# A shifted-window transformer block: the first score pass loads its queries and its block-diagonal keys from the second pass's pages in DRAM

## The chip, the cores and the metric

The kernel runs on one core of a Trainium2 chip. The metric is the device time of one launch in microseconds (us). The engines are TensorE (PE, with its weight loads as PEld), VectorE (DVE), ScalarE (ACT), GpSimd (POOL) and SyncE (SP), which here issues every DMA. There are 16 DMA engines, and all of SP's DMAs go into one queue.

## The reference

The input is a batch of 32 images of 96 channels and 56 x 56 pixels, in float32. One Swin block is computed:

```
f = layernorm(x over channels) * g1 + b1, rolled by (-3, -3)
win = windows of 7 x 7 = 49 tokens            (64 windows per image)
q, k, v = win @ w_qkv + b_qkv                 (12 heads of 8 channels)
attn = softmax(q k^T / sqrt(8) + mask)        (mask: -100 between regions of the rolled image)
f = x + roll back(attn v @ w_proj + b_proj)
out = f + gelu((layernorm(f) * g2 + b2) @ w_fc1 + b_fc1) @ w_fc2 + b_fc2
```

## The kernel before

**Bands and steps.** A band is one row of 8 windows, 392 tokens (`TOK`). There are 256 bands. Work is software-pipelined by hand: in step t each stage works on band t plus its own offset (line 60): `LOAD` 9, `ORDER` 7, `TURN` 6, `BACK` 5, `QK` 4, `KEYS` 3, `VALUES`, `SCORE` and `STACK` 2, `PROB` 0, `WEIGH` -1. Every engine runs its own list of stages per step, one list for odd and one for even t (`step` of each engine), and engines meet only at semaphores. A loop of 32 steps runs seven times, and the other steps are written out (`steps`, line 181).

**Two score passes.** Scores are computed twice. The first pass (`scores`, L404 to L421; PSUM banks from A) has query tokens in rows and key tokens in columns and multiplies high fp16 parts only; the DVE takes row maxima from it (`maxima`, L736). The maxima are transposed, and ACT copies them to `mrow` (L650), which a DMA writes into one row of `qbd`. The second pass (`shifted`, L423 to L437; banks from B) has key tokens in rows. It multiplies stacked high and low parts and subtracts mask and maximum in the same matmul. ACT exponentiates its result (L623), and `weighted` (L439) multiplies it with `vbd`.

A matmul covers a quad of 4 heads and one window at a time: 49 query tokens against 4 x 49 key columns. Heads are kept apart by a block-diagonal operand: in `kbd` the rows of head h are non-zero only in the columns of head h. In the first pass of before the stationary operand is `nat`: 96 channel rows of queries, and 4 mask rows from 96 on. `kbd` has the same 96 rows and 4 mask rows for 12 heads. Both are 128 partitions deep with zeros for the rest.

**From projections to score operands.** `queries_keys` (PE, L495) leaves q and k of band t+4 in PSUM. ACT writes the high parts to `nat` at the end of step t (`queries_keys_high`, L638 to L644, semaphore `qk_high`). The DVE writes the low parts (`queries_keys_low`, L778, `qk_low`): in an odd step as the third operation, in an even one after the first maximum, each time for the band of the step before. SP then writes them to DRAM in `save_parts` (L283): L292 the high keys into the diagonal of the zeroed image `k_image` (DRAM, two of them), L293 both parts of q and k into `stack_pages`, and L294 the high parts a second time, so that a stack of 3 pieces per channel (high, low, high or high, high, low) stands in each page. In the next step `key_blocks` (L258) waits for the image and loads it whole into `kbd` (L264: 96 rows of 9,408 bytes, zeros with it), for `scores` one step later. `stacks` (L266) loads `kst` and `qbd` from `stack_pages` for the second pass.

**SP's order in a step** is `load_x` (L256), `key_blocks` (L264), in odd steps two `store_y` (L300), then `stacks` (L272, and L274 four times), `maxima` (L281), `save_parts` (L292 to L294). SP works through it in order; the wait for `qk_low` in `save_parts` is for the DVE of the following step. `alone` (L203) only counts.

**PE's order** is in `step` (L567). In an odd step `shifted`(0) and `values` (L400) stand before `scores`(0); in an even step `scores`(0) is first. `scores`(0) waits for `key_in` (L409).

**Start.** The DVE zeroes the operand tiles (L703 to L709), then SP loads constants (L224; 28 DMAs, among them two writes of zeroed `kbd` to the images at L243), and all engines wait for the last of them.

Of the kernel before, what the change touches and what calls it, by code (L numbers as in the profile page):

```python
# [31 lines left out]
F16 = mybir.dt.float16  # L32
# [5 lines left out]
HD = C // NH  # L38
# [11 lines left out]
MASK0, MAXROW = C, C + 4  # L50
CH = 4 * L
# [11 lines left out]
N_CONST = 9 + 5 + 6 + 5 + 3  # L63
# [28 lines left out]
def build(nc, x, g1, b1, wqkv, bqkv, wproj, bproj, g2, b2, wfc1, bfc1, wfc2, bfc2,  # L92
# [7 lines left out]
    with ctx:  # L100
# [24 lines left out]
        nat = sb("nat", [FULL, 5, 4, TOK], F16)  # L125
        kst = sb("kst", [FULL, 3, QUADS, TOK], F16)
        qbd = sb("qbd", [FULL, 2, NH, TOK], F16)
        kbd = sb("kbd", [FULL, 2, NH, TOK], F16)
        vbd = sb("vbd", [FULL, 4, PAIRS * NH, 2, HD + 1])
# [17 lines left out]
        parts_out = [stack_pages[n, TOK:TOK + 2 * side].rearrange("(s c m t) -> c s m t", s=2, m=3, t=TOK)[:, :, 0:2, :] for n in range(4)]  # L147
        high_out = [stack_pages[n].rearrange("(s r) -> s r", s=2)[:, 0:side].rearrange("s (c m t) -> c s m t", m=3, t=TOK)[:, :, 0, :] for n in range(4)]
        k_pages = nc.dram_tensor("k_image", [2, NH, HD * NH * TOK + TOK], F16, kind="Internal").ap()
        k_image = [k_pages[n].rearrange("h r -> (h r)")[0:C * NH * TOK].rearrange("(c g t) -> c g t", g=NH, t=TOK) for n in range(2)]  # L150
        k_diagonal = [k_pages[n, :, 0:HD * NH * TOK].rearrange("h (d r) -> h d r", d=HD)[:, :, 0:TOK] for n in range(2)]
# [7 lines left out]
        image_out = [sem(f"image_out{n}") for n in range(2)]  # L159
# [4 lines left out]
        NAT_OUT, STACK_IN = 2 * 16, 5 * 16  # L164
# [42 lines left out]
        def nat_slot(b):  # L207
            return 4 if b.last() else b.c % 4

        def kst_slot(b):  # L210
            return 2 if b.last() else b.c % 2
# [10 lines left out]
        def _(sp):  # L222
# [19 lines left out]
            for n in range(2):  # L242
                const(k_image[n], kbd[0:C, n, :, :])  # L243
                const(kbd[MASK0:MAXROW, n, :, :], rows_d[2, 0:4])
                const(qbd[MASK0:MAXROW, n, :, :], rows_d[2, 0:4])
            for n in range(5):
                const(nat[MASK0:MAXROW, n, 0, :], rows_d[n // 4, 0:4, 0, :])
            for n in range(3):
                const(kst[MASK0:MAXROW + 1, n, :, :], rows_d[n // 2, :, 0:QUADS, :])
# [8 lines left out]
            def key_blocks(b):  # L258
                n = b.c % 2
                wait(sp, s_made, b.count(QUADS, -QUADS))  # L260
                alone(sp)
                sp.wait_ge(image_out[n], b.used(2, 16))
                alone(sp)
                sp.dma_start(kbd[0:C, n, :, :], k_image[n]).then_inc(key_in[n], 16)  # L264

            def stacks(b):  # L266
# [3 lines left out]
                sp.wait_ge(nat_out[n], b.used(4, NAT_OUT))  # L270
                alone(sp)
                sp.dma_start(kst[0:C, kst_slot(b), :, :], k_stack[n].rearrange("(c a) m t -> (a m) c t", c=QUADS)).then_inc(stack_in[n], 16)  # L272
# [10 lines left out]
            def save_parts(b):  # L283
# [3 lines left out]
                wait(sp, key_in[b.c % 2], b.step(-2).used(2, 16))  # L287
                alone(sp)
                sp.wait_ge(qk_low, b.count(1, 1))
                alone(sp)  # L290
                parts = nat[0:C, nat_slot(b), :, :]
                sp.dma_start(k_diagonal[b.c % 2], parts[:, 2, :]).then_inc(image_out[b.c % 2], 16)  # L292
                sp.dma_start(parts_out[n], parts.rearrange("c (s m) t -> c s m t", s=2)).then_inc(nat_out[n], 16)  # L293
                sp.dma_start(high_out[n], parts[:, 0:4:2, :]).then_inc(nat_out[n], 16)  # L294
# [76 lines left out]
        def _(pe):  # L371
# [32 lines left out]
            def scores(t, u):  # L404
# [3 lines left out]
                if u == 0:  # L408
                    pe.wait_ge(key_in[b.c % 2], b.used(2, 16))  # L409
# [6 lines left out]
                for p in range(PAIRS):  # L416
                    for w in range(2):
                        toks = slice((2 * p + w) * L, (2 * p + w + 1) * L)
                        last = nc.tensor.matmul(psum[W1 * w:W1 * w + L, A + p // 2, p % 2 * CH:(p % 2 + 1) * CH],  # L419
                                                nat[:, nat_slot(b), 0, toks], kbd[:, b.c % 2, 4 * u:4 * u + 4, toks], start=True, stop=True)  # L420
# [452 lines left out]
```

## Time and profile before

| | before |
|---|---|
| three runs | 3273.74, 3298.38, 3312.33 us |
| median | 3298.38 us |
| the profiled execution | 3292.7 us, its span 3290.8 us |
| busy: PE, PEld, DVE, ACT, POOL | 89%, 71%, 74%, 63%, 44% |
| mean granted clock of TensorE, of full speed | 0.977 |
| DMA moved | 573.07 MB |
| loads of `kbd` | 256 of 882.0 KB, 6.8 us median from issue to landing |

Busy is the time in which an engine executed at least one instruction, as a share of the span. Waits of the bottleneck engine are what a change can take away. The profiled execution has its own time; sums over its rows are made against 3292.7 us.

### The profile page before, as it was taken

The numbers are of one execution on the slowest core, as the hardware profiler recorded it, in microseconds if no ns is written. First come the engines' busy times: TensorE is split into PE (matmuls) and PEld (weight loads), VectorE is DVE, ScalarE is ACT, GpSimd is POOL, SyncE is SP. The second block draws the span as 40 slices with busy tenths as digits, with TensorE's granted clock in tenths as the row PEclk, the third lists the DMA queues.
The fourth block names the chain that finished last, engine by engine and source line by source line (L and its number), as shares of the span: only waits on it lengthen the run. The fifth ranks groups of instructions, "written<-read, shape, count | busy, mean of one in ns | idle before, by whom it ended". The sixth has DMA issues, their size and how long they took to land.

```text
span 3290.8 us, 136960 instructions
## 1 busy us (share of the span) xinstructions
PE 2926.7 (89%) x53060; PEld 2338.7 (71%) x53060; DVE 2430.1 (74%) x7208; ACT 2070.5 (63%) x3208; POOL 1453.1 (44%) x1832
## 2 busy tenths in 40 slices
PE   1789999899998899989998999989999899999997
PEld 0677777777776777767776777767777777777775
DVE  5677777677776777767777777767777677777775
ACT  0366666566666666656666666666666566666664
POOL 2444444344444444444444444444444444444444
PEclk9799999899999999999999999999999999999999
DMA  1667777677776777767777777767767677777772
GB/s 40 170 170 187 182 190 188 164 172 184 185 175 171 176 183 193 186 164 186 189 180 175 177 178 194 184 164 186 187 168 186 164 188 179 188 186 192 182 183 71
DMA packets 409846, 573.07 MB, mean 174 GB/s; under 512 B 58376, under 2 KB 384350, under 8 KB 384365
## 3 DMA queue, kind: packets, MB, share of 16 engines
q1 hardware_dynamic: 409148, 563.72, 68.9%
q8 instruction: 444, 7.27, 1.0%
q14 instruction: 254, 2.07, 0.2%
HBM read 385.92 MB, written 175.21 MB: 171 GB/s over the span
## 4 chain that ended last, share of the span: by engine, by line
PE 40%; DMA 26%; issue 11%; SPq 10%; DVE 9%; ACT 4%; POOL 0%; DVEq 0%; POOLq 0%; ACTq 0%
DMA kbd<-k_image 24%; PE psum L451 10%; PE psum L384 9%; PE psum L419 5%; PE psum L435 4%; PE psum L492 4%; PE psum L477 4%; DVE nat L778 3%; DVE nmax L736 3%; ACT xfh L635 3%; SPq L292 2%; SPq L256 2%; SPq L293 2%; SPq L294 2%; PE psum L527 2%
## 5 line engine op out<-in xcount | busy, mean ns | idle before, releaser
L623 ACT ACTIVATE probs<-psum 113x784 f32<-113x784 f32 x768 | 632.2, 823 | 847.4 <-PE psum L435 844.2
L736 DVE TENSOR_REDUCE nmax<-psum 113x16 f32<-113x784 f32 x768 | 745.6, 971 | 316.5 <-PE psum L419 316.2
L347 POOL TENSOR_SCALAR ve<-mv 98x8 f32<-98x8 f32 x264 | 64.1, 243 | 1687.7 <-DVE mv L765 1687.7
L451 PE MATMUL psum<-vbd,probs 128*49 128x18 f32 x24576 | 656.5, 199 | 26.3 <-issue 25.5
L451 PEld LDWEIGHTS psum<-vbd,probs 128*49 128x49 f32 x24576 | 646.0, 128 | 32.0 <-issue 31.7
L419 PE MATMUL psum<-kbd,nat 128*49 128x196 f16 x6144 | 412.5, 254 | 114.5 <-DMA kbd<-k_image 103.8
L435 PE MATMUL psum<-qbd,kst 128*49 128x196 f16 x6144 | 413.7, 254 | 67.0 <-DVE xfl L771 45.5
L354 POOL TENSOR_TENSOR rs<-ve,half 98x8 f32<-98x8 f32 x264 | 439.5, 1665 | 0.0
L760 DVE BATCH_NORM_STATS2 st<-tok 98x6 f32<-98x96 f32 x2112 | 363.7, 245 | 80.8 <-ACT tok L630 67.3
L359 POOL TENSOR_TENSOR xn<-xn,rs 98x768 f32<-98x768 f32 x264 | 387.8, 1469 | 72.7 <-POOL rs L354 72.7
L419 PEld LDWEIGHTS psum<-kbd,nat 128*49 128x49 f16 x6144 | 269.4, 105 | 209.2 <-DMA kbd<-k_image 134.4
L771 DVE TENSOR_TENSOR xfl<-psum,xfh 96x784 f16<-96x784 f32 x264 | 256.1, 970 | 190.5 <-ACT xfh L635 188.5
L350 POOL TENSOR_TENSOR xn<-tok,mv 98x768 f32<-98x768 f32 x264 | 389.1, 1474 | 0.2 <-POOL ve L347 0.2
L435 PEld LDWEIGHTS psum<-qbd,kst 128*49 128x49 f16 x6144 | 243.4, 105 | 166.5 <-issue 129.8
L564 PE MATMUL psum<-hid,w 128*96 128x392 f32 x1024 | 359.7, 494 | 0.9 <-ACT hid L666 0.9
L644 ACT ACTIVATE nat<-psum 96x784 f16<-96x784 f32 x256 | 209.7, 819 | 129.2 <-PE psum L384 129.2
L564 PEld LDWEIGHTS psum<-hid,w 128*96 128x96 f32 x1024 | 167.5, 164 | 171.8 <-issue 170.5
L492 PE MATMUL psum<-ident,xn 98*96 98x98 f32 x2112 | 228.0, 252 | 65.3 <-issue 57.4
L617 ACT ACTIVATE vbd<-psum 49x384 f32<-49x384 f32 x512 | 261.0, 510 | 10.8 <-PE psum L400 4.4
L635 ACT ACTIVATE xfh<-psum 96x784 f16<-96x784 f32 x264 | 215.2, 815 | 78.6 <-PE psum L492 78.3
L492 PEld LDWEIGHTS psum<-ident,xn 98*96 98x96 f32 x2112 | 189.6, 128 | 91.4 <-issue 81.6
L666 ACT ACTIVATE hid<-psum 96x784 f32<-96x784 f32 x256 | 209.8, 819 | 60.5 <-PE psum L384 55.7
(83 smaller groups left out, 5343.1 us busy)
## 6 DMA issues: line engine op xcount, KB each, us to landing
kbd<-k_image SPq DMA_DIRECT2D x256, 882.0 KB, 6.8
stack_pages<-nat SPq DMA_DIRECT2D x256, 294.0 KB, 3.0
kst<-stack_pages SPq DMA_DIRECT2D x256, 220.5 KB
qbd<-stack_pages SPq DMA_DIRECT2D x1024, 55.1 KB
stack_pages<-nat SPq DMA_DIRECT2D x256, 147.0 KB, 3.7
xr<-in_x_dram SPq DMA_DIRECT2D x224, 147.0 KB, 3.6
out_dram<-yr SPq DMA_DIRECT2D x224, 147.0 KB, 6.3
k_image<-nat SPq DMA_DIRECT2D x256, 73.5 KB
```

Of the source, the lines that this page charges most:

```text
L350: nc.gpsimd.tensor_tensor(xn[:, n, :, :], tok[:, n, :, :, :].rearrange("t k p c -> t (k p) c"), mv[:, n, :, 0:1].to_broadcast(wide_by_toke ...
L354: nc.gpsimd.tensor_tensor(rs[:, n, :], ve[:, n, :], half[0:PT, :], ALU.pow).then_inc(root_done, 1)
L359: nc.gpsimd.tensor_tensor(xn[:, n, :, :], xn[:, n, :, :], rs[:, n, :].rearrange("t (g a) -> t g a", a=1).to_broadcast(wide_by_token), ALU. ...
L419: last = nc.tensor.matmul(psum[W1 * w:W1 * w + L, A + p // 2, p % 2 * CH:(p % 2 + 1) * CH], nat[:, nat_slot(b), 0, toks], kbd[:, b.c % 2, ...
L435: last = nc.tensor.matmul(psum[W1 * w:W1 * w + L, B + p // 2, p % 2 * CH:(p % 2 + 1) * CH], kst[:, kst_slot(b), u, toks], qbd[:, b.c % 2, ...
L451: last = nc.tensor.matmul(dst[:, :, h, :], probs[:, b.c % 2, h // 4, p, h % 4 * L:(h % 4 + 1) * L], vbd[:, b.c % 4, p * NH + h, :, :], sta ...
L492: last = nc.tensor.transpose(psum[0:C, B + kind, p * PT:(p + 1) * PT], xn[:, b.c % 2, kind * PAIRS + p, :], ident[0:PT, 0:PT])
L564: last = nc.tensor.matmul(psum[0:C, D + n, 0:TOK], w2[:, m, :], hid[:, b.c % 2, m, :], start=m == 0, stop=m == 1)
L623: nc.scalar.activation(probs[0:PR, b.c % 2, u, :, :].rearrange("j (g q) k -> j g (q k)", g=2), psum[0:PR, B:B + 2, 0:2 * CH], ACT.Exp).the ...
L635: nc.scalar.activation(xfh[0:C, b.c % 4, :, :], psum[0:C, B:B + 2, 0:TOK], ACT.Copy).then_inc(n_high, 1)
L736: nc.vector.tensor_reduce(dst, psum[0:PR, A:A + 2, 0:2 * CH].rearrange("i g (q h j) -> i g q h j", q=2, j=L), axis=AX.X, op=ALU.max, negat ...
L760: last = nc.vector.bn_stats(st[:, n, g, :], tok[:, n, g // PAIRS, g % PAIRS, :])
```

## The change

The first pass works on the 32 channel rows of one quad. A new tile `qst` (3 slots x 3 quads) holds in rows 0 to 31 the high queries of a quad, and in rows 32 to 35 (`QUAD` is 32) the mask rows. `kbd` keeps its shape, but rows 0 to 31 hold the four diagonal blocks of each quad. The image of key blocks in DRAM, its zeroing at the start, its write in each step and its load are gone. Instead `key_blocks` reads the high parts from `stack_pages`: one DMA for `qst` (73.5 KB) and four for `kbd` (8 rows x 3 quads, 18.4 KB each). The matmuls have the same number, shape and depth (128 rows).

`save_parts` issues the write of the high parts when `qk_high` has come, and then waits for `qk_low` to write both parts. `key_blocks` waits for the write of the high parts only (`high_out`). `nat` has 4 slots instead of 5 and no mask rows. ACT's write of `nat` no longer waits for scores, since no matmul reads `nat`. The start has 24 constant DMAs.

```diff
@@ -122,10 +123,11 @@
         st, mv = sb("st", [PT, 2, 2 * PAIRS, 6]), sb("mv", [PT, 2, 2 * PAIRS, 2])
         ve, rs = sb("ve", [PT, 2, 2 * PAIRS]), sb("rs", [PT, 2, 2 * PAIRS])
         xfh, xfl = sb("xfh", [FULL, 4, 2, TOK], F16), sb("xfl", [FULL, 4, 2, TOK], F16)
-        nat = sb("nat", [FULL, 5, 4, TOK], F16)
+        nat = sb("nat", [C, 4, 4, TOK], F16)
         kst = sb("kst", [FULL, 3, QUADS, TOK], F16)
         qbd = sb("qbd", [FULL, 2, NH, TOK], F16)
         kbd = sb("kbd", [FULL, 2, NH, TOK], F16)
+        qst = sb("qst", [FULL, 3, QUADS, TOK], F16)
         vbd = sb("vbd", [FULL, 4, PAIRS * NH, 2, HD + 1])
         nmax = sb("nmax", [PR, 2, NH * PAIRS])
         mrow = sb("mrow", [NH * PAIRS, 2, PT], F16)
...
@@ -144,11 +146,8 @@
         stack_pages = nc.dram_tensor("stack_pages", [4, 2 * (side + 3 * TOK)], F16, kind="Internal").ap()
         q_stack = [stack_pages[n, 0:side].rearrange("(c m t) -> c m t", m=3, t=TOK) for n in range(4)]
         k_stack = [stack_pages[n, TOK + side:TOK + 2 * side].rearrange("(c m t) -> c m t", m=3, t=TOK) for n in range(4)]
-        parts_out = [stack_pages[n, TOK:TOK + 2 * side].rearrange("(s c m t) -> c s m t", s=2, m=3, t=TOK)[:, :, 0:2, :] for n in range(4)]
-        high_out = [stack_pages[n].rearrange("(s r) -> s r", s=2)[:, 0:side].rearrange("s (c m t) -> c s m t", m=3, t=TOK)[:, :, 0, :] for n in range(4)]
-        k_pages = nc.dram_tensor("k_image", [2, NH, HD * NH * TOK + TOK], F16, kind="Internal").ap()
-        k_image = [k_pages[n].rearrange("h r -> (h r)")[0:C * NH * TOK].rearrange("(c g t) -> c g t", g=NH, t=TOK) for n in range(2)]
-        k_diagonal = [k_pages[n, :, 0:HD * NH * TOK].rearrange("h (d r) -> h d r", d=HD)[:, :, 0:TOK] for n in range(2)]
+        both_parts = [stack_pages[n, TOK:TOK + 2 * side].rearrange("(s c m t) -> c s m t", s=2, m=3, t=TOK)[:, :, 0:2, :] for n in range(4)]
+        high_parts = [stack_pages[n].rearrange("(s r) -> s r", s=2)[:, 0:side].rearrange("s (c m t) -> c s m t", m=3, t=TOK)[:, :, 0, :] for n in range(4)]
 
         consts_in, filled, rows_one, vbd_zero, vbd_ones = sem("consts_in"), sem("filled"), sem("rows_one"), sem("vbd_zero"), sem("vbd_ones")
         psum_clear, weights_wide, weights_high, weights_set = sem("psum_clear"), sem("weights_wide"), sem("weights_high"), sem("weights_set")
...
@@ -156,12 +155,12 @@
 
         x_in = [sem(f"x_in{n}") for n in range(8)]
         nat_out = [sem(f"nat_out{n}") for n in range(4)]
-        image_out = [sem(f"image_out{n}") for n in range(2)]
+        high_out = [sem(f"high_out{n}") for n in range(4)]
         key_in = [sem(f"key_in{n}") for n in range(2)]
         stack_in = [sem(f"stack_in{n}") for n in range(4)]
         max_in = [sem(f"max_in{n}") for n in range(2)]
         y_out = [sem(f"y_out{n}") for n in range(8)]
-        NAT_OUT, STACK_IN = 2 * 16, 5 * 16
+        STACK_IN, KEY_IN = 5 * 16, 5 * 16
         X_IN = [16] * 7 + [2 * 16]
 
         passed = sem("passed")
...
@@ -204,10 +203,7 @@
 
             engine.sem_inc(passed, 1)
 
-        def nat_slot(b):
-            return 4 if b.last() else b.c % 4
-
-        def kst_slot(b):
+        def masked_slot(b):
             return 2 if b.last() else b.c % 2
 
         def odd(t):
...
@@ -240,12 +236,10 @@
                 column(n, v)
 
             for n in range(2):
-                const(k_image[n], kbd[0:C, n, :, :])
-                const(kbd[MASK0:MAXROW, n, :, :], rows_d[2, 0:4])
+                const(kbd[QUAD:QUAD + 4, n, :, :], rows_d[2, 0:4])
                 const(qbd[MASK0:MAXROW, n, :, :], rows_d[2, 0:4])
-            for n in range(5):
-                const(nat[MASK0:MAXROW, n, 0, :], rows_d[n // 4, 0:4, 0, :])
             for n in range(3):
+                const(qst[QUAD:QUAD + 4, n, :, :], rows_d[n // 2, 0:4, 0:QUADS, :])
                 const(kst[MASK0:MAXROW + 1, n, :, :], rows_d[n // 2, :, 0:QUADS, :])
             sp.wait_ge(consts_in, 16 * N_CONST)
 
...
@@ -259,17 +253,20 @@
                 n = b.c % 2
                 wait(sp, s_made, b.count(QUADS, -QUADS))
                 alone(sp)
-                sp.wait_ge(image_out[n], b.used(2, 16))
-                alone(sp)
-                sp.dma_start(kbd[0:C, n, :, :], k_image[n]).then_inc(key_in[n], 16)
+                sp.wait_ge(high_out[b.c % 4], b.used(4, 16))
+                alone(sp)
+                sp.dma_start(qst[0:QUAD, masked_slot(b), :, :], q_stack[b.c % 4].rearrange("(c a) m t -> m a c t", c=QUADS)[0]).then_inc(key_in[n], 16)
+                for h in range(4):
+                    sp.dma_start(kbd[HD * h:HD * (h + 1), n, h:NH:4, :],
+                                 k_stack[b.c % 4].rearrange("(c h d) m t -> h m d c t", c=QUADS, h=4)[h, 2]).then_inc(key_in[n], 16)
 
             def stacks(b):
                 n = b.c % 4
                 wait(sp, p_made, b.count(QUADS, -QUADS))
                 alone(sp)
-                sp.wait_ge(nat_out[n], b.used(4, NAT_OUT))
-                alone(sp)
-                sp.dma_start(kst[0:C, kst_slot(b), :, :], k_stack[n].rearrange("(c a) m t -> (a m) c t", c=QUADS)).then_inc(stack_in[n], 16)
+                sp.wait_ge(nat_out[n], b.used(4, 16))
+                alone(sp)
+                sp.dma_start(kst[0:C, masked_slot(b), :, :], k_stack[n].rearrange("(c a) m t -> (a m) c t", c=QUADS)).then_inc(stack_in[n], 16)
                 for h in range(4):
                     sp.dma_start(qbd[HEAD * h:HEAD * (h + 1), b.c % 2, h:NH:4, :],
                                  q_stack[n].rearrange("(c h d) m t -> h (d m) c t", c=QUADS, h=4)[h]).then_inc(stack_in[n], 16)
...
@@ -284,14 +281,12 @@
                 n = b.c % 4
                 wait(sp, stack_in[n], b.step(-4).used(4, STACK_IN))
                 alone(sp)
-                wait(sp, key_in[b.c % 2], b.step(-2).used(2, 16))
-                alone(sp)
+                sp.wait_ge(qk_high, b.count(1, 1))
+                alone(sp)
+                sp.dma_start(high_parts[n], nat[:, n, 0:4:2, :]).then_inc(high_out[n], 16)
                 sp.wait_ge(qk_low, b.count(1, 1))
                 alone(sp)
-                parts = nat[0:C, nat_slot(b), :, :]
-                sp.dma_start(k_diagonal[b.c % 2], parts[:, 2, :]).then_inc(image_out[b.c % 2], 16)
-                sp.dma_start(parts_out[n], parts.rearrange("c (s m) t -> c s m t", s=2)).then_inc(nat_out[n], 16)
-                sp.dma_start(high_out[n], parts[:, 0:4:2, :]).then_inc(nat_out[n], 16)
+                sp.dma_start(both_parts[n], nat[:, n, :, :].rearrange("c (s m) t -> c s m t", s=2)).then_inc(nat_out[n], 16)
 
             def store_y(b):
                 sp.wait_ge(y_made, b.count(1, 1))
...
@@ -406,7 +401,7 @@
                 if not has(b):
                     return
                 if u == 0:
-                    pe.wait_ge(key_in[b.c % 2], b.used(2, 16))
+                    pe.wait_ge(key_in[b.c % 2], b.used(2, KEY_IN))
                     if odd(t):
                         if has(t.step(QK - 1)):
                             pe.wait_ge(qk_low, t.step(QK - 1).count(1, 1))
...
@@ -417,7 +412,7 @@
                     for w in range(2):
                         toks = slice((2 * p + w) * L, (2 * p + w + 1) * L)
                         last = nc.tensor.matmul(psum[W1 * w:W1 * w + L, A + p // 2, p % 2 * CH:(p % 2 + 1) * CH],
-                                                nat[:, nat_slot(b), 0, toks], kbd[:, b.c % 2, 4 * u:4 * u + 4, toks], start=True, stop=True)
+                                                qst[:, masked_slot(b), u, toks], kbd[:, b.c % 2, 4 * u:4 * u + 4, toks], start=True, stop=True)
                 last.then_inc(s_made, 1)
 
             def shifted(t, u):
...
@@ -638,10 +633,9 @@
                 b = t.step(QK)
                 at = D if odd(t) else A
                 act.wait_ge(qk_made, b.count(1, 1))
-                wait(act, nat_out[b.c % 4], b.step(-4).used(4, NAT_OUT))
-                wait(act, image_out[b.c % 2], b.step(-4).used(2, 16))
-                wait(act, s_made, b.count(QUADS, -3 * QUADS))
-                nc.scalar.activation(nat[0:C, nat_slot(b), 0:4:2, :], psum[0:C, at:at + 2, 0:TOK], ACT.Copy, scale=1 / GAIN).then_inc(qk_high, 1)
+                wait(act, nat_out[b.c % 4], b.step(-4).used(4, 16))
+                wait(act, high_out[b.c % 4], b.step(-4).used(4, 16))
+                nc.scalar.activation(nat[0:C, b.c % 4, 0:4:2, :], psum[0:C, at:at + 2, 0:TOK], ACT.Copy, scale=1 / GAIN).then_inc(qk_high, 1)
 
             def max_rows(t):
                 b = t.step(SCORE)
...
@@ -699,9 +693,9 @@
         @block.vector
         def _(dve):
 
-            for a in (kbd, qbd):
+            for a in (kbd, qbd, qst):
                 nc.vector.memset(a[:, :, :, :], 0.0)
-            for a in (wide, wide1, wp, w2, xfh, xfl, oT, hid, nat, kst, probs):
+            for a in (wide, wide1, wp, w2, xfh, xfl, oT, hid, kst, probs):
                 last = nc.vector.memset(a[FILL:FULL], 0.0)
             last.then_inc(filled, 1)
             dve.wait_ge(filled, 1)
```

## Rows read from the trace of the kernel before

**Rows 1.** The page: span and busy time of each engine
```profile
span 3290.8 us, 136960 instructions
PE 2926.7 (89%) x53060; PEld 2338.7 (71%) x53060; DVE 2430.1 (74%) x7208; ACT 2070.5 (63%) x3208; POOL 1453.1 (44%) x1832
```

**Rows 2.** Waits, whole span: total us, times, longest us
```profile
PE psum L419 <- DMA kbd<-k_image: 103.8, 111, 3.3
PE psum L435 <- DVE xfl L771: 45.5, 10, 6.7
```

**Rows 3.** Waits of SP's own queue, whole span
```profile
SPq L205 <- DVE nat L778: 736.7, 256, 17.6
SPq L205 <- ACT mrow L650: 182.8, 118, 4.0
SPq L205 <- DMA k_image<-nat: 112.0, 97, 3.1
```

**Rows 4.** Timeline of an even step and the next odd one: start us, us, instruction
```profile
1526.11 0.82 ACT L644 ACTIVATE nat<-psum 96x784 f16<-96x784 f32 x1 [0.18 <-PE psum L384]
1528.59 0.96 DVE L778 SCALAR_TENSOR_TENSOR nat<-psum,nat 96x784 f16<-96x784 f32 x1
1529.64 0.80 SPq L292 DMA_DIRECT2D k_image<-nat  x1
1530.49 0.51 SPq L293 DMA_DIRECT2D stack_pages<-nat  x1
1531.83 0.34 SPq L256 DMA_DIRECT2D xr<-in_x_dram  x1
1532.43 0.33 SPq L264 DMA_DIRECT2D kbd<-k_image  x1
1536.82 0.58 SPq L281 DMA_DIRECT2D qbd<-mrow  x1
1539.33 0.21 PE L400 MATMUL psum<-wl,xfh 128*49 128x96 f16 x2
1539.86 0.53 PE L419 MATMUL psum<-kbd,nat 128*49 128x196 f16 x8 [0.32 <-DMA kbd<-k_image]
...
1550.14 0.53 PE L419 MATMUL psum<-kbd,nat 128*49 128x196 f16 x8
```

**Rows 5.** Instructions of L274, L264 and L292: nanoseconds, least, median, most
```profile
L274 SPq DMA_DIRECT2D qbd<-stack_pages x1024: 291/427/1636, 97.8 to 3234.1; - x171
L264 SPq DMA_DIRECT2D kbd<-k_image x256: 303/320/1361, 84.5 to 3221.1; - x128
L292 SPq DMA_DIRECT2D k_image<-nat x256: 770/797/892, 81.9 to 3218.8; - x128
```

**Rows 6.** Issue to landing: first L264, then L294, then L256
```profile
DMA to landing us min/median/max: 5.8/6.8/8.9
DMA to landing us min/median/max: 2.8/3.7/5.7
DMA to landing us min/median/max: 1.8/3.3/6.0
```

**Rows 7.** Timeline of the start: start, duration
```profile
17.71 3.33 DVE L705 MEMSET nat<- 32x3920 uint32 x1 [0.77 <-issue]
33.76 0.43 SPq L224 DMA_DIRECT2D k_image<-kbd  x1
35.61 1.47 SPq L224 DMA_DIRECT2D k_image<-kbd  x1
38.81 2.98 SPq L224 DMA_DIRECT2D nat<-in_rows_dram  x5
41.83 0.97 SPq L224 DMA_DIRECT2D kst<-in_rows_dram  x3
```

**Rows 8.** Windows: start:end, length, PE busy, granted clock, DMA share, GB/s
```profile
200.00:3000.00 2800.00, 2566.34 (x46977) 0.98 0.73 181
2400.00:2412.50 12.50, 11.02 (x187) 0.73 0.89 220
```

More of the change, by code:

```diff
@@ L50 @@
 MASK0, MAXROW = C, C + 4
+QUAD = C // QUADS
 CH = 4 * L
@@ L62 @@
 HIDDEN, RESULT, STORE = (-5, -4), (-6, -5), (-7, -6)
-N_CONST = 9 + 5 + 6 + 5 + 3
+N_CONST = 9 + 5 + 4 + 6
 class Band:
@@ L435, in shifted @@
                         last = nc.tensor.matmul(psum[W1 * w:W1 * w + L, B + p // 2, p % 2 * CH:(p % 2 + 1) * CH],
-                                                kst[:, kst_slot(b), u, toks], qbd[:, b.c % 2, 4 * u:4 * u + 4, toks], start=True, stop=True)
+                                                kst[:, masked_slot(b), u, toks], qbd[:, b.c % 2, 4 * u:4 * u + 4, toks], start=True, stop=True)
                 last.then_inc(p_made, 1)
@@ L776, in queries_keys_low @@
                 dve.wait_ge(qk_high, b.count(1, 1))
-                parts = nat[0:C, nat_slot(b), :, :]
+                parts = nat[0:C, b.c % 4, :, :]
                 nc.vector.scalar_tensor_tensor(out=parts[:, 1:4:2, :], in0=psum[0:C, at:at + 2, 0:TOK], scalar=1 / GAIN, in1=parts[:, 0:4:2, :],
```

## The prediction, made before the changed kernel ran

> **What bounds the kernel now.** I read the busy times first: PE is busy 2926.7 of 3290.8 us, and DVE, the next, 2430.1 [rows 1]. So PE sets the time, and only its 364.1 us of idleness and its own work can change the result. The change leaves PE's work alone: as many matmuls of the same shape over the same 128 rows. So I read what PE waited for [rows 2]. The largest single item is the load of `kbd`, 103.8 us in 111 waits, 0.94 us each. The 45.5 us in 10 waits for the DVE's low parts, up to 6.7 us each, are mostly the seven loop returns, and stay. What PE has at stake here is 103.8 us, 3.2% of the span.
>
> Then the timeline around one such wait [rows 4]. ACT has the high parts of band t+4 at 1526.93. The DVE has the low parts at 1529.55. Only then does SP write: the image write takes 0.80 us to issue, the page write 0.51, then come the second high write and the load of x, and the load of `kbd` goes out at 1532.43. It lands at about 1539.82, when PE has been free since 1539.54. The chain from low parts to landed keys is 10.3 us against 10.0 us that PE's own work lasts. SP's waits [rows 3] say the same from the other side: 112.0 us in 97 waits are spent on the image write's landing, before the big load can even be issued.
>
> **The change, part by part.**
>
> Removed and added in SP's queue, per band. The image write goes (0.797 us median) and the `kbd` load (0.320) [rows 5]. Five loads come. For each of the four `kbd` pieces the nearest row is L274, also one of four DMAs that each take one head in four out of these pages: 0.427 us median, 0.291 to 1.636 [rows 5]; I take the median. For `qst`, a load of all its rows at once, I take the 0.320 of L264. New issue 4 x 0.427 + 0.320 = 2.03 us against 1.12 removed, so +0.91 us per band, and about 0.05 us between issues for three more DMAs, as between the rows of the timeline: +1.06 us, 271 us over 256 bands. SP's three largest waits sum to 1031.5 us [rows 3], so this is covered: SP stays idle for over 700 us. If that cover were gone, all of it would be paid, see the third rival.
>
> The load, timed on the rows 4. High parts: ready at 1526.93, SP is waiting, write issued at about 1527.0, landed by 3.7 us later (L294's median; 2.8 to 5.7) [rows 6] at 1530.7. Low parts at 1529.55; page write issued 1529.64 to 1530.15. From its end to the load of x now pass 0.83 us with L294's issue in them; I keep them whole, so x goes out at 1530.98 to 1531.32, and `key_blocks` starts near 1531.6 (0.26 us on, as now). The high write has landed by then, so the new wait costs nothing. The last of the five loads is issued at 1531.6 + 0.37 + 3 x 0.48 = 1533.4. Its landing is not in the trace. Bounds: 1.8 us, the fastest load of x, and 8.9, the slowest of the whole image [rows 6]. I take 3.3, the median of the x loads, which carry 147.0 KB each, as much as the five together. Landed at 1536.7, against 1539.54 when PE arrives: 2.8 us spare, where now 0.3 are missing. With the 6.8 of today's load it would be 1540.2 and as late as now; with 8.9, 2.8 us late. In the even steps SP is busy longer: the maxima go out at 1536.82 for 0.58 [rows 4], in future about 1 us later, so the high write is issued near 1538.4 and lands at 1542.1. There the high write is the last to come, and `key_blocks` waits for it. The last load is issued near 1543.9 and lands at 1547.2, against PE's even scores at 1550.14. So both parities have 2.8 us spare or a little more. Queued behind that wait are in odd steps the stores, the stacks and the maxima; none is due before the step after next.
>
> Term 1: the waits for `kbd`, -103.8 us. What stays of them: at the seven loop returns SP itself is late, and a wait there can outlast the cover. I leave 7 times half of the longest wait (3.3), 12 us. Bounds: all 103.8 gained, or none. I take -92.
>
> Behind PE's wait nothing else was hidden that I can find: in the odd step the DVE's maxima come as PE's scores end, where the DVE is idle until PE delivers; PE does `weighted` in between.
>
> Traffic. 882.0 KB and 73.5 KB per band become 147.0 KB. DMA engines are busy 0.73 of the time [rows 8] and would fall well below 0.6. PE does not wait for bandwidth as such, so I count nothing for that; the instruction fetch, which may profit, is in a rival.
>
> Term 2: the start [rows 7]. The DVE's memset of `nat` goes (3.33 + 0.77 us), and one of `qst` comes, 1.5 us by its 1764 words against 3920. SP issues two image writes less (0.43 + 1.47), five masks of `nat` less (2.98) and three of `qst` more (0.97 by `kst`). That is -2.6 and -3.9 us, all on the path, since every engine waits for the last constant. Two image writes less in the queue are worth 0 to 3 us. Sum -6.5 to -9.5, I take -7.
>
> Term 3: the clock. Its mean is 0.98 over 2800 us [rows 8]: 4% of the time at 1.2 instead of 2.4 GHz, 112 us, costing at most 56. Most low stretches follow the loop returns; the one at 2400 does not [rows 8]. Bounds 0 and -56; PE's waits for `kbd` are 29% of its idleness and short, so I take -5.
> The Trainium skill (TensorE: Matmul & The Clock Gate, "HAM oscillation — how this bites in real kernels") says that waits for DMA between bursts of matmuls throttle the clock again, after which work runs at half rate. Read that way, the low stretches would be a price of waits like these, and the sum would use up to all of the 56 us: that is the second rival. The trace speaks for little of it, as 111 such waits go with few low stretches.
>
> **Sum:** 3292.7 - 92 - 7 - 5 = 3189 us. The profiled execution (3292.7) lies 0.2% under the median of the three runs (3298.38), which go from 3273.74 to 3312.33; I let the sum stand for the new median.
>
> **Rivals.**
>
> *The loads land as late as now.* Five DMAs behind the page write of 294 KB instead of one: their fixed parts count, not their bytes. It needs a landing of over 6.1 us after the last issue. For it: 6.8 is what the load has today, and x loads have taken 6.0. Against it: it moves a sixth of the bytes. Then only the start is gained: 3292.7 - 7 = 3286. The Trainium skill (DMA: Bandwidth & Descriptors, "Measured", under Bandwidth) advises to batch DMAs to 1 MiB and calls transfers under 64 KB descriptor-dominated, which speaks for this rival; x's small loads, at 3.3 us, speak against. Chance 0.12.
>
> *More than the waits.* Less idleness keeps the clock up, and lighter queues shorten the instruction fetch stalls. 3292.7 - 104 - 9 - 40 = 3140, the 40 being most of the clock's 56. Chance 0.10.
>
> *SP becomes the bound.* It holds every DMA, and if the four small loads cost more than L274's, SP uses up its 1031 us. What it may spend per piece: per band it has 1031.5 / 256 = 4.03 us idle and 1.12 us removed, and gives 0.32 for `qst` and 0.15 between issues; the other 4.68 us over four pieces are 1.17 us each. Above that each 0.1 us costs 102 us over 1024 pieces: at 1.4 us the time would be 3292.7 - 7 + 236 = 3522. For it: issues of 1.36 and 1.64 us do occur, and the waits in SP's queue can't all be moved to where they are needed. Against: the median is 0.427. With partial queueing the result is merely slower by a few per cent. Chance 0.08, slower.
>
> *Half is given back.* PE, no longer held, meets the DVE's first or second maximum of the odd step or a fetch stall that the wait had covered. 3292.7 - 52 - 7 = 3234. Chance 0.12.
>
> **Numbers.** The forecast, 3189 us, has 0.58. Range: the low end is the second rival less a quarter of the spread of the three runs (38.6 us), 3130; the high end is the half gain plus 1% for runs, 3266. That leaves out the first and third rival. Within 1% of the median, 3265 to 3331, is what I can't tell from no change. Faster: 0.58 + 0.12 + 0.10 = 0.80; same 0.12; slower 0.08.
>
> **What would show it.** Right: PE's wait for `kbd` or `qst` under 20 us in total; SP's waits still over 600 us, with no large one for the high write; the last `kbd` load lands 3 to 4 us after its issue; first matmul of the constants near 40 us instead of 47.5; DMA bytes near 359 MB (573 less 256 times 955.5 KB and plus 256 times 147 KB, at 1,024 bytes a KB, less the two images at the start). Wrong: a landing over 6 us; L264's successors with a median issue over 1 us; PE's waits for the maxima of L736 in place of those for the keys; a mean clock under 0.97.

## The result and the profile after

| | before | after |
|---|---|---|
| median | 3292.15 us (4 runs, 3273.74 to 3312.33) | 3062.89 us (4 runs, 3061.32 to 3065.84) |
| span of the profiled execution | 3290.8 us | 3061.1 us |
| mean granted clock | 0.977 | 0.992 |
| DMA moved | 573.07 MB | 359.37 MB |

The ratio is 0.9303, with a 95% interval of 0.9246 to 0.9361. The change is worth 229 us, more than twice the 109 us of the forecast, and lies under the low end of the range. Medians here are over all runs of a kernel, ratios over its fast ones alone (within 1.5% of its fastest), which leaves out one run each of e1_bulk and e10_bulk_half, five of the ten of e9_bulk_first, and two of the thirteen of before that go with e9 to e11.

The page after, span and busy time, as in [rows 1]:

```profile
span 3061.1 us, 137479 instructions
PE 2862.6 (94%) x53060; PEld 2299.2 (75%) x53060; DVE 2424.3 (79%) x7208; ACT 2076.6 (68%) x3208; POOL 1454.5 (48%) x1832
```

PE's idle time went from 364.1 to 198.5 us, and its busy time fell by 64.1 us, for the same 53060 matmuls. The chain that ended last now is PE for 87% of the span.

PE's waits after (total us, times, longest us), which answer to [rows 2], and its stalls, which stand mostly within groups of equal matmuls:

```profile
PE psum L371 <- DMA kst<-in_rows_dram: 38.1, 1, 38.1
PE psum L487 <- issue: 57.1, 120, 1.0
PE psum L430 <- DVE xfl L765: 23.2, 10, 2.8
PE psum L446 <- issue: 9.0, 18, 1.0
PE psum L414 <- issue: 4.2, 7, 2.5
PE psum L430 <- issue: 2.8, 5, 0.7
```

The same view before had, beside [rows 2]:

```profile
PE psum L376 <- DMA kst<-in_rows_dram: 47.5, 1, 47.5
PE psum L492 <- issue: 57.4, 121, 1.0
PE psum L451 <- issue: 25.5, 38, 1.5
PE psum L435 <- issue: 12.3, 19, 2.1
PE psum L419 <- issue: 6.6, 9, 1.5
PE psum L400 <- issue: 1.7, 4, 0.7
```

(L451, L435, L419 and L400 of before are L446, L430, L414 and L395 after.) No wait for keys is left, and three other things became smaller. "Issue" in the middle of a group of equal matmuls is no semaphore, since the program has none there: PE waits for nothing but its own next instruction. ("Issue" at the head of a group, as in L487, can be a semaphore that the profile did not match; e7_back_early shows that one to be such.) SP's own waits after:

```profile
SPq L204 <- DVE nat L772: 473.9, 254, 5.4
SPq L204 <- ACT nat L638: 222.7, 166, 15.0
SPq L204 <- ACT mrow L644: 167.1, 115, 3.0
SPq L204 <- DMA stack_pages<-nat: 5.8, 13, 0.9
```

They still sum to 869.5 us, and the new wait for the high write costs 5.8. Against [rows 4], the timeline of an even step (start, duration):

```profile
1498.21 0.32 SPq L286 DMA_DIRECT2D stack_pages<-nat  x1
1499.45 0.96 DVE L772 SCALAR_TENSOR_TENSOR nat<-psum,nat 96x784 f16<-96x784 f32 x1
1500.51 0.30 SPq L289 DMA_DIRECT2D stack_pages<-nat  x1
1501.15 1.23 SPq L250 DMA_DIRECT2D xr<-in_x_dram  x1
1502.64 0.30 SPq L258 DMA_DIRECT2D qst<-stack_pages  x1
1502.99 1.36 SPq L260 DMA_DIRECT2D kbd<-stack_pages  x4
...
1510.09 0.51 PE L414 MATMUL psum<-kbd,qst 128*49 128x196 f16 x8
```

The loads are all issued at 1504.35, 5.7 us before PE begins the scores. The last step of their semaphore that the trace has comes at 1505.74, 1.4 us after the last issue. The four pieces of `kbd` cost 0.300 us each to issue and the high write lands in 2.0 us; L260, and then the landing of L286:

```profile
L260 SPq DMA_DIRECT2D kbd<-stack_pages x1024: 264/300/1815, 73.9 to 2989.7; - x171
DMA to landing us min/median/max: 1.9/2.0/4.2
```

One loop return in each kernel, from the DVE's side: the first instruction of the DVE after it, with its idle time in brackets, before and after.

```profile
1412.26 0.62 DVE L785 SCALAR_TENSOR_TENSOR f<-psum,vec,xw 96x392 f32<-96x392 f32 x1 [7.26 <-issue]
934.50 0.62 DVE L779 SCALAR_TENSOR_TENSOR f<-psum,vec,xw 96x392 f32<-96x392 f32 x1 [3.40 <-issue]
```

PE waits at L435 (L430 after) for this DVE: 6.0 to 6.7 us at each of the six returns of before, 2.5 to 2.8 after.

Two windows (start:end, length, PE busy, granted clock, DMA share, GB/s), as in [rows 8]:

```profile
200.00:3000.00 2800.00, 2704.58 (x50651) 1.00 0.47 122
2400.00:2412.50 12.50, 9.88 (x185) 0.86 0.29 74
```

**Where the 229.7 us of the spans went:**

| | before | after | gain |
|---|---|---|---|
| wait for keys | 103.8 | 0 | 103.8 |
| L435, now L430, waiting for the DVE's low parts, six long ones at loop returns | 45.5 | 23.2 | 22.3 |
| "issue" stalls in L451, L435, L419 and L400 | 46.1 | 16.0 | 30.1 |
| first matmul of the start | 47.5 | 38.1 | 9.4 |
| PE's other idle time (the rest of 364.1 and 198.5) | 121.2 | 121.2 | 0 |
| PE busy | 2926.7 | 2862.6 | 64.1 |

The waits for keys, which I had forecast, are less than half.

### The profile page after: what moved, and what is told of

It is laid out like the page before. It is cut to its first block, busy times and chain, and to the rows that moved or that the text cites. A ratio compares the mean times of both kernels' runs of the same rounds, so it can differ in the third digit from the quotient of the medians.

```text
span 3061.1 us, 137479 instructions
## 1 busy us (share of the span) xinstructions
PE 2862.6 (94%) x53060; PEld 2299.2 (75%) x53060; DVE 2424.3 (79%) x7208; ACT 2076.6 (68%) x3208; POOL 1454.5 (48%) x1832
## 2 busy tenths in 40 slices
DMA packets 414727, 359.37 MB, mean 117 GB/s; under 512 B 63455, under 2 KB 413985, under 8 KB 414012
## 3 DMA queue, kind: packets, MB, share of 16 engines
q1 hardware_dynamic: 414028, 350.01, 43.7%
## 4 chain that ended last, share of the span: by engine, by line
PE 87%; issue 5%; ACT 5%; DVE 2%; POOL 1%; SPq 0%; DMA 0%; POOLq 0%; DVEq 0%; ACTq 0%
PE psum L446 18%; PE psum L379 16%; PE psum L559 11%; PE psum L430 10%; PE psum L414 8%; PE psum L472 7%; PE psum L487 6%; PE psum L532 5%; ACT probs L618 4%; PE psum L522 3%; PE psum L395 2%; PE psum L511 1%; DVE st L754 1%; POOL rs L349 0%; DVE xfl L765 0%
## 5 line engine op out<-in xcount | busy, mean ns | idle before, releaser
L446 PE MATMUL psum<-vbd,probs 128*49 128x18 f32 x24576 | 644.2, 198 | 9.8 <-issue 9.0
L446 PEld LDWEIGHTS psum<-vbd,probs 128*49 128x49 f32 x24576 | 634.4, 126 | 14.1 <-issue 13.3
L430 PE MATMUL psum<-qbd,kst 128*49 128x196 f16 x6144 | 405.1, 251 | 36.3 <-DVE xfl L765 23.2
L414 PE MATMUL psum<-kbd,qst 128*49 128x196 f16 x6144 | 401.4, 250 | 7.6 <-issue 4.2
L430 PEld LDWEIGHTS psum<-qbd,kst 128*49 128x49 f16 x6144 | 238.8, 104 | 142.1 <-issue 103.0
L414 PEld LDWEIGHTS psum<-kbd,qst 128*49 128x49 f16 x6144 | 265.0, 104 | 85.3 <-issue 80.6
L559 PEld LDWEIGHTS psum<-hid,w 128*96 128x96 f32 x1024 | 167.4, 164 | 171.9 <-issue 170.6
L487 PE MATMUL psum<-ident,xn 98*96 98x98 f32 x2112 | 227.8, 252 | 64.9 <-issue 57.1
L487 PEld LDWEIGHTS psum<-ident,xn 98*96 98x96 f32 x2112 | 189.3, 128 | 91.0 <-issue 81.1
L772 DVE SCALAR_TENSOR_TENSOR nat<-psum,nat 96x784 f16<-96x784 f32 x256 | 245.7, 960 | 0.0
## 6 DMA issues: line engine op xcount, KB each, us to landing
qst<-stack_pages SPq DMA_DIRECT2D x256, 73.5 KB
kbd<-stack_pages SPq DMA_DIRECT2D x1024, 18.4 KB
```

The lines of the kernel that those rows point to most:

```text
L430: last = nc.tensor.matmul(psum[W1 * w:W1 * w + L, B + p // 2, p % 2 * CH:(p % 2 + 1) * CH], kst[:, masked_slot(b), u, toks], qbd[:, b.c % ...
L446: last = nc.tensor.matmul(dst[:, :, h, :], probs[:, b.c % 2, h // 4, p, h % 4 * L:(h % 4 + 1) * L], vbd[:, b.c % 4, p * NH + h, :, :], sta ...
L487: last = nc.tensor.transpose(psum[0:C, B + kind, p * PT:(p + 1) * PT], xn[:, b.c % 2, kind * PAIRS + p, :], ident[0:PT, 0:PT])
L559: last = nc.tensor.matmul(psum[0:C, D + n, 0:TOK], w2[:, m, :], hid[:, b.c % 2, m, :], start=m == 0, stop=m == 1)
```

## The experiments

All are timed against runs of the kernel before on the same chip. Here is the summary; the edits and expectations follow. "Stalls" is the sum of PE's "issue" waits at the four lines of the table above, "return" the wait of the line that was L435 for the DVE's low parts. The changed kernel was timed apart from the experiments, so differences to its 3062.89 us can be between chips; before has medians of 3299.11 us beside e1 to e4, 3288.76 beside e5 to e8 and 3287.62 beside e9 to e11. Clock, share, waits and stalls are of one profiled execution each. That of e9_bulk_first is the fastest of its ten (3238.02 to 3305.81 us), so its waits and stalls may be low.

| | median us | ratio to before (95%) | clock | queue 1 share | wait for keys | stalls | return |
|---|---|---|---|---|---|---|---|
| before | - | 1 | 0.977 | 68.9% | 103.8 | 46.1 | 45.5 |
| after | 3062.89 | 0.930 (0.925 to 0.936) | 0.992 | 43.7% | 0 | 16.0 | 23.2 |
| e3_early | 3172.39 | 0.966 (0.959 to 0.972) | 0.984 | 71.6% | 12.3 | 46.4 | 36.6 |
| e4_late | 3061.21 | 0.930 (0.925 to 0.936) | 0.993 | 43.5% | 0 | 11.8 | 25.1 |
| e1_bulk | 3353.60 | 1.014 (1.003 to 1.024) | 0.959 | 70.4% | 0 | 171.9 | 41.4 |
| e2_small | 3447.37 | 1.045 (1.038 to 1.052) | 0.944 | 72.0% | 0 | 222.5 | 43.2 |
| e9_bulk_first | 3284.61 | 1.001 (0.997 to 1.005) | 0.975 | 74.6% | 91.9 | 23.8 | 35.5 |
| e10_bulk_half | 3169.61 | 0.963 (0.956 to 0.970) | 0.980 | 66.4% | 0 | 66.6 | 35.0 |
| e11_bulk_last | 3406.94 | 1.034 (1.026 to 1.042) | 0.949 | 65.5% | 24.3 | 184.7 | 24.6 |

**e3_early**: the kernel before with the early write alone. In `save_parts`:

```diff
-                sp.wait_ge(qk_low, b.count(1, 1))
+                sp.wait_ge(qk_high, b.count(1, 1))
                 alone(sp)
                 parts = nat[0:C, nat_slot(b), :, :]
                 sp.dma_start(k_diagonal[b.c % 2], parts[:, 2, :]).then_inc(image_out[b.c % 2], 16)
+                sp.wait_ge(qk_low, b.count(1, 1))
+                alone(sp)
```

> The kernel before with one part of the change alone: the high keys are written to the image when qk_high has come, ahead of the low parts; image and whole-image load stay. The load of kbd then goes out 0.8 us earlier and without the image wait. Theory W: PE's waits for the keys nearly vanish and stalls and clock recover with them: about 3100. Theory T: the waits go (at most -104 us), loop returns, fetch stalls and clock stay as they were: 3190 to 3230, clock 0.977 to 0.985.

Measured 3172.39 us. PE's waits in this kernel:

```profile
PE psum L421 <- DMA kbd<-k_image: 12.3, 18, 2.7
PE psum L437 <- DVE xfl L773: 36.6, 10, 5.2
PE psum L453 <- issue: 25.7, 35, 1.8
```

91.5 us of waiting for keys are gone although the 882 KB load is still there. The stalls of L451 stayed (25.7 against 25.5), and the return column fell by 9 us only. The clock rose to 0.984. So the early write by itself removes most of the waits, and neither of my two theories has it whole: stalls are not the waits' doing, but part of the clock seems to be. (SP still waits 66.1 us for the image write, which I had expected to end.)

**e4_late**: the changed kernel with the high parts written after `qk_low`.

```diff
-                sp.wait_ge(qk_high, b.count(1, 1))
+                sp.wait_ge(qk_low, b.count(1, 1))
                 alone(sp)
                 sp.dma_start(high_parts[n], nat[:, n, 0:4:2, :]).then_inc(high_out[n], 16)
-                sp.wait_ge(qk_low, b.count(1, 1))
-                alone(sp)
                 sp.dma_start(both_parts[n], ...).then_inc(nat_out[n], 16)
```

> The changed kernel with one part undone: the high parts are written after qk_low, still ahead of both parts, and the small loads wait for that. The landing of the high write (2.0 us in the changed kernel) comes into the chain. By my account of the slack (key loads issued 6 us ahead of PE's scores) PE hardly waits: 3060 to 3080 by theory T. If the early write is a main part of the gain, PE waits over 50 us for kbd and the time is over 3110.

Measured 3061.21 us, the same as the changed kernel. SP now waits 93.9 us for the write, and PE for no key:

```profile
SPq L204 <- DMA stack_pages<-nat: 93.9, 163, 2.5
```

Of the two parts of the change either one takes nearly all waits for keys away; with the small loads the early write is worth nothing.

**e1_bulk**: the changed kernel with a load of the old size, which nobody needs, behind the key loads.

```diff
+        spare = sb("spare", [C, NH, TOK], F16)
...
+        spare_page = nc.dram_tensor("spare_page", [C, NH, TOK], F16, kind="Internal").ap()[:, :, 0:TOK]
...
+            const(spare_page, qbd[0:C, 0, :, :])
...
                     sp.dma_start(kbd[HD * h:HD * (h + 1), n, h:NH:4, :], ...).then_inc(key_in[n], 16)
+                wait(sp, spare_in, b.count(16))
+                alone(sp)
+                sp.dma_start(spare[:, :, :], spare_page).then_inc(spare_in, 16)
```

> The changed kernel, with a load of 882 KB per band (96 rows of 9,408 bytes, as the old load of kbd) into a tile that nobody reads, issued behind the key loads. It is an addition, the output stays. Theory T (traffic): the big load was what made instruction fetch slow, so that the loop returns held the engines for 6 us and the clock fell behind them. Then PE's stalls between equal matmuls go back from about 16 to about 45 us, the six long waits of L430 from 2.6 to over 5 us each, the clock from 0.99 towards 0.98, and the time from 3063 to 3130 to 3170. Theory W (waits): PE's waits for the keys themselves lowered the clock and shifted the fetches; since key loads stand ahead of the added load, the time stays under 3085 with a clock over 0.99.

Measured 3353.60 us: 291 us more, far beyond either range, and 1.4% slower (0.3 to 2.4) than the kernel before with about the same bytes. PE waits for no key; it stalls on itself:

```profile
PE psum L453 <- issue: 75.1, 66, 2.9
PE psum L437 <- DVE xfl L772: 41.4, 10, 6.1
PE psum L437 <- issue: 40.1, 27, 2.6
PE psum L421 <- issue: 33.5, 17, 2.7
PE psum L402 <- issue: 23.2, 14, 2.1
```

One of these stalls close up, first PE's timeline:

```profile
1508.05 0.44 PE L437 MATMUL psum<-qbd,kst 128*49 128x196 f16 x6 [2.60 <-issue]
```

and the DMA queues (packets, MB, share of 16 engines), first from 1498 to 1505 us, then from 1505 to 1506:

```profile
q1 hardware_dynamic: 1124, 1.67, 102.3%
...
q1 hardware_dynamic: 185, 0.26, 76.8%
q8 instruction: 1, 0.02, 6.5%
```

For 7 us SP's queue fills all 16 engines and the instruction queue gets nothing in. The next packet of the instruction queue starts at 1505.48, as the backlog runs out, and ends at 1506.53; PE, which stands from 1505.45, goes on at 1508.05.

The whole traces show the same. Of the 119 stalls of over 0.3 us at the four lines, 118 end 1.0 to 1.9 us after a packet of queue 8 has ended, and so do all 56 of before. There are 255 stretches of 3 us or more in which queue 1 keeps the engines over 90% busy (in steps of 0.5 us), 45% of the span. Only 4 of the 444 packets of queue 8 start in the first half of such a stretch; 59 start in its last sixth and 94 in the microsecond behind it. When each fetch was asked for, the trace does not show.

Nearly the whole price is found in PE's row: of 285.2 us between the spans, stalls are 155.9, the return column 18.2 and PE's busy time 109.0 (2971.6 against 2862.6), the last with the clock at 0.959.

**e2_small**: as e1_bulk, but the same bytes in pieces of 784 bytes.

```diff
-        spare_page = nc.dram_tensor("spare_page", [C, NH, TOK], ...
+        spare_page = nc.dram_tensor("spare_page", [C, NH, TOK + 8], ...
```

> As e1_bulk, but the source rows are pitched, so that the same 882 KB come in pieces of 784 bytes (12 per row). If the fetches queue behind long packets (theory P, packets), this costs clearly less than e1_bulk: under 3090. If the sum of traffic counts (theory T), it costs as much or more, 3130 to 3190. By theory W nothing, under 3085.

Measured 3447.37 us, 94 more than e1_bulk and above every range of the expectation. Long packets in front of the fetch are not the cause; small pieces are worse.

**e9_bulk_first, e10_bulk_half, e11_bulk_last**: place and size of the added load. In e9 its three lines stand ahead of the load of `qst`, in e11 at the end of `stacks`; in e10 it is

```diff
-                sp.dma_start(spare[:, :, :], spare_page).then_inc(spare_in, 16)
+                sp.dma_start(spare[0:48, :, :], spare_page[0:48]).then_inc(spare_in, 16)
```

> e1_bulk with the added 882 KB load issued ahead of the five key loads instead of behind them: the same DMAs and bytes, one place earlier in SP's queue. In e1_bulk a fetch of PE's instructions (queue 8) landed only when SP's backlog had drained, and PE stood 2.6 us. Theory B (backlog meets fetch): what counts is where the backlog ends against PE's dense stretch at the start of a step, so the time changes clearly, towards e3_early: under 3280. Theory S (sum of traffic): same bytes, same time as e1_bulk, 3354 within 30 us. Key loads land 4 us later, which the slack of 5 us should hide; if not, PE waits for kbd show it.

> e1_bulk with half the load (48 rows of 9,408 bytes, 441 KB). If the stalls grow in proportion to the bytes, 3063 + 145 = 3210. If only a backlog that reaches into the dense stretch hurts, far less: 3070 to 3120.

> e1_bulk with the added load issued behind the loads of kst and qbd, later still by 2 to 4 us. Theory B: the backlog now ends after the next step has begun, deeper in the dense stretch, so it is as bad as e1_bulk or worse, over 3330, with PE's stalls between equal matmuls over 200 us in total. Theory S: 3354 within 30.

Measured: first 3284.61 us, behind the keys 3353.60, last 3406.94. First and last ran on one chip, with ratios of 1.001 (0.997 to 1.005) and 1.034 (1.026 to 1.042): the same DMAs and bytes differ by 122 us by their place in SP's queue, so the sum of traffic does not set the price. The one between, e1_bulk, ran on another chip, and its interval (1.003 to 1.024) touches that of e9_bulk_first. In the profile of e9_bulk_first the stalls are nearly gone; the keys are late instead:

```profile
PE psum L421 <- DMA kbd<-stack_pages: 91.9, 108, 5.0
PE psum L453 <- issue: 16.7, 27, 1.4
```

The slack of 5 us did not hide the bulk. My expectation of under 3280 is missed by 5 us, which is inside the spread of the ten runs and decides nothing. e11_bulk_last came out over 3330 as theory B had it, but with stalls of 184.7 us, not over 200. Half the load costs 107 of the 291 us, between my two ranges, less than its share.

**e5_before_long_loop, e6_after_long_loop**: one line in either kernel.

```diff
-TURNS = 4
+TURNS = 8
```

> The kernel before with a loop of 64 steps (TURNS 8) instead of 32: two returns instead of six, the rest of the steps written out. A return holds PE 6.3 us there and a stretch at half clock of 6.8 to 13.7 us follows. If both are the return's price, 4 returns less are worth 4 x (6.3 + 3.4 to 5) = 39 to 45 us: 3255. If the half clock comes from elsewhere (the waits for keys), 25 us: 3270.

> The changed kernel with the loop of 64 steps. A return holds PE 2.6 us there, and 3.4 us at half clock follow in some: 4 x (2.6 + 1) = 14 us less, 3049. Rival: at this size the written-out code costs as much as the returns, no change within 5 us.

Measured 3257.33 us against 3288.76 us for before (0.988, 0.981 to 0.995), 31 us less, and 3052.58 us, 10 us less than the 3062.89 of the changed kernel. The interval of e5 is 18 to 63 us, so it does not tell 25 from 39 to 45. In e5 the wait for the DVE's low parts fell from 45.5 to 20.7 us, so a return costs 6 us, while the mean clock rose only from 0.977 to 0.980. By the trace's clock records 14 us at half clock go with its two returns, where before had 65 with six, but other places in the steady part have 89 where before had 34. So fewer returns alone do not cure the clock.

**e7_back_early**: the largest wait that is left in the changed kernel, a condition that asks for more than is needed.

```diff
                 if odd(t):
-                    wait(pe, gelu_done, t.step(HIDDEN[1]).count(1, 1)) if has(t.step(HIDDEN[1])) else None
+                    wait(pe, gelu_done, t.step(HIDDEN[0]).count(1, 1)) if has(t.step(HIDDEN[0])) else None
```

> The changed kernel, where in odd steps the back transposes (bank B) wait only for the first GELU, which reads B, and not for the second, which reads bank A. The 0.47 us wait in each odd step is 59 us in total, the largest wait of PE that is left. If PE alone is the bound, up to 59 us less: 3004 to 3015. If ACT's or DVE's copies behind the transposes are paced by the second GELU anyway, PE meets its next wait (for the projection's input or in the next step) and less than 15 us come: over 3048.

Measured 2985.22 us (6 runs, 2982.68 to 2986.06; ratio to before 0.908, 0.903 to 0.912): 78 us less than the changed kernel, 21 more than the wait itself (57.1). The page, and the lines of L487 in the changed kernel and here:

```profile
span 2983.1 us, 137486 instructions
PE 2836.7 (95%) x53060; PEld 2298.2 (77%) x53060; DVE 2423.8 (81%) x7208; ACT 2060.3 (69%) x3208; POOL 1452.8 (49%) x1832
```

```profile
L487 PE MATMUL psum<-ident,xn 98*96 98x98 f32 x2112 | 227.8, 252 | 64.9 <-issue 57.1 <-POOL xn L354 4.9 <-ACT hid L660 3.0
```

```profile
L487 PE MATMUL psum<-ident,xn 98*96 98x98 f32 x2112 | 225.5, 250 | 5.9 <-POOL xn L354 5.9
```

PE's idle time fell by 52.1 us (198.5 to 146.4) and its busy time by 25.9 us at the same clock (0.992 and 0.993). At most 3 us of that are the clock's by its records (48 and 42 us at half clock). Matmuls overlap: the 2112 of L487 last 250 ns each and keep PE busy for 225.5 us. One that comes after a wait does not overlap with the one before, which is the likely reason why a removed wait gives back more than its idle time, here 25.9 us for 120 waits, 0.2 us each. No row shows that reason apart.

**e8_both**: e6 and e7 together.

> e6 and e7 together. If their gains add: 3063 less the sum of both, near 2995. It is the candidate for a version that beats both kernels.

Measured 2971.89 us (0.9035 of before, 0.898 to 0.909), 13 us under e7. The gains add. It is the fastest version of this study.

## Why the prediction was wrong

**Bottleneck and first term: right.** PE's waits for the keys were what the change removes directly, and all 103.8 us of them went; I had taken 92, leaving 12 for the loop returns, where none was left. (A loop that runs seven times returns six times; I had counted seven.) SP did not become the bound: the four pieces cost 0.300 us each, where I had 0.427, and 869.5 us of waiting stayed with it. The high write landed after 2.0 us, not 3.7. From the last issue to PE's scores 5.7 us pass, where I had 6.1, but the loads landed 1.4 us after it instead of my 3.3, as far as the trace shows. So about 4.3 us were spare, not 2.8, and the sign "lands 3 to 4 us after its issue" did not come.

**The start:** 9.4 us on PE, where I had 7.

**The step that failed** is "Traffic", with its sentence "PE does not wait for bandwidth as such, so I count nothing for that; the instruction fetch, which may profit, is in a rival". The price of the traffic was in the trace in two places that I had not priced. One is the 46.1 us of "issue" stalls inside groups of equal matmuls. The other is the 6.0 to 6.7 us of each return of the loop, which I wrote off with the words "and stay". The removed load takes 30.1 us from the first and 22.3 from the second: 52.4 us where I had nothing. e1_bulk shows the cause from the other side: with the load put back where PE waits for no key, the stalls rise to 171.9 us and the returns to 41.4. At before's return at 1407.40 the DMA engines are 94% busy from 1405 to 1409 us and the first packet of the other instruction queue (14) starts at 1409.23; the DVE goes on at 1412.26. e3_early shows that the early write does not do it: with the load in place the stalls stay (46.4) and the return column is 36.6, where the changed kernel has 16.0 and 23.2.

**The third term, the clock, was mis-sized.** I took 5 us of at most 56. Mean clocks of 0.977 and 0.992 are 151 and 49 us at half clock (twice the missing share times the span), so up to 51 us came from there. That is the better part of the 64.1 us by which PE's busy time fell. The rest is probably the refill after a wait, for which e7_back_early gives a price: 111 waits of [rows 2] at 0.2 us are about 22 us, an estimate, and with 51 somewhat more than the 64.1 that there are. My reason, that 111 waits go with few low stretches, was true and not enough. Between 200 us and the end of the steady part the clock records of before have twelve stretches at half clock: four (27 us) right after a wait for keys, two (7 us) after a stall, and six (65 us) that begin during the six returns. After, there are four left, 14 us in all, at returns. The low stretches at the returns shrank with the returns, which I had taken to stay; the first 200 us went from 48 to 21 us at half clock as well. The clock goes with the stalls as well: it is 0.959 in e1_bulk, where PE waits for no key at all and only stalls, 0.984 in e3_early, where most waits are gone and the stalls not, and 0.992 in the changed kernel, with no wait for keys and 16.0 us of stalls.

**The rivals.** "More than the waits" had the right mechanisms, clock and fetch, with 40 us for them, where stalls, returns and busy time brought 116.5, and only 0.10; it stood at 3140, and the time lies 77 us below that too. "The loads land as late as now", "SP becomes the bound" and "half is given back" did not happen. The Trainium skill (TensorE: Matmul & The Clock Gate, "HAM oscillation — how this bites in real kernels") says that waits for DMA between bursts of matmuls throttle the clock; the traces agree in part, since four low stretches of before begin right after a wait for keys and none is left in the steady part of the changed kernel outside the returns. The Trainium skill (DMA: Bandwidth & Descriptors, "Measured", under Bandwidth) advises large DMAs, by measurements of DMAs that GpSimd issues; here, where SP issues them, five small ones with a sixth of the bytes were far better than one large one. That small pieces cost at equal bytes is seen in e2_small against e1_bulk (94 us), there for pieces within one DMA.

**What stays open.** Why the same 882 KB cost 109 us in the kernel before (e3_early against the changed kernel, which differ in more than the load) and 291 in e1_bulk. The 101.4 us between the spans of e3_early and the changed kernel are PE's busy time 37.3, stalls 30.4, the return column 13.4, waits for keys 12.3 and the start 9.4, less 1.4 elsewhere. The place in SP's queue accounts for part of the difference, e9_bulk_first against e1_bulk: 69 us by the medians, about 40 by the ratios to before. That the rest is five loads more in the queue ahead of the bulk is a guess that was not measured. Why e10_bulk_half costs 107 us, between both of my ranges, is open too.

## What to carry to other kernels

The profile lists instruction packets (queues 8 and 14) among the packets of the same DMA engines that carry data. Where PE stalls in the middle of a group of equal matmuls ("issue"), look at the instruction queue's packets in that stretch: when a large load keeps all engines busy while PE runs through many short instructions, the stall is likely a price of that load, and so is what the clock loses after it. A transfer that PE does not wait for is then not free (up to 344 us here), and a removed wait can be worth more than its idle time (78 us for 57.1 in e7_back_early).

## What was not expected of the hardware

- While one queue filled the 16 DMA engines for 7 us (102.3%) no instruction packet moved, though instructions have queues of their own; over the whole of e1_bulk 4 of 444 started in the first half of such a stretch. PE went on 1.0 to 1.9 us after the packet had ended.
- A loop return costs PE 6.0 to 6.7 us in a kernel that moves 573 MB and 2.5 to 2.8 us in one that moves 359 MB.
- The same added load cost 222, 291 or 344 us by its place in SP's queue (against 3062.89 us; the second on another chip than the others).
- A wait of 0.47 us, once per odd step, cost PE 0.65 us (78 us over 120 such waits in the trace).
